# A decoder layer on one core: the expert routing moved from a block of its own into the attention phase, and the sorted rows fetched by GpSimd through a table

## The reference, cut to what matters

```
x = x + attn(layernorm(x))            # 2 x 1024 tokens, width 256, 16 heads of 64, one shared k/v head, causal
x = x + xattn(layernorm(x), ctx)      # 77 context rows for each batch, 16 heads of 16
z = layernorm(x)
logits = z @ w_router                 # 4 experts
e = argmax(softmax(logits))           # one expert for each token
gate, value = split(z @ w_v[e])       # 256 -> 2 x 1024
x = x + (gate * sigmoid(gate) * value) @ w_proj[e]   # 1024 -> 256
```

## Time and profile before

| | |
|---|---|
| time of three runs, median (lowest to highest) | 998.96 us (996.46 to 1001.12) |
| the profiled execution's own time | 1001.04 us |
| its span, first to last instruction | 999.3 us |
| busy share of the span: PE, DVE, ACT, POOL | 88%, 61%, 56%, 20% |
| mean granted TensorE clock | 0.939 of full |

### The profile page before, as it was taken

How to read it: one execution, slowest core, us unless ns; L and a number is a source line. 1 busy time by engine, 2 the same in 40 slices (tenths; PEclk the granted TensorE clock), 3 DMA queues, 4 the chain that set the end, 5 groups by cost and what they waited for, 6 DMA issues and landing times.

```text
span 999.3 us, 14240 instructions
## 1 busy us (share of the span) xinstructions
PE 882.3 (88%) x4366; PEld 669.0 (67%) x4366; DVE 612.9 (61%) x1417; ACT 562.5 (56%) x1112; POOL 203.9 (20%) x220
## 2 busy tenths in 40 slices
PE   4699898999999897999989999999760299999997
PEld 2467676777777675776776777777550178888885
DVE  4667758667858677668766778778766133323231
ACT  1478667677867577667758678768442022222221
POOL 3212321302112121212313020201103401111111
PEclk9699999999999999999989999999955599999999
DMA  8300000020000000000000003200232201010100
GB/s 283 71 1 1 1 1 1 1 85 1 1 2 0 1 2 0 2 1 0 2 1 1 1 1 107 63 1 1 85 127 72 81 1 32 20 32 21 32 17 9
DMA packets 19175, 29.01 MB, mean 29 GB/s; under 512 B 2079, under 2 KB 15648, under 8 KB 19104
## 3 DMA queue, kind: packets, MB, share of 16 engines
q1 hardware_dynamic: 17008, 22.73, 7.5%
q0 software_dynamic: 1680, 4.21, 1.2%
q10 hardware_dynamic: 416, 1.18, 0.3%
HBM read 21.41 MB, written 7.10 MB: 29 GB/s over the span
## 4 chain that ended last, share of the span: by engine, by line
PE 49%; DVE 6%; issue 5%; POOL 3%; ACT 2%; DMA 1%; DVEq 0%; ACTq 0%; POOLq 0%
PE W L1418 7%; PE S L1395 6%; PE O L1395 5%; PE O L1235 3%; PE O L1232 3%; PE S L1217 3%; PE S L1216 3%; PE O L1233 3%; PE W L1306 3%; PE W L1348 3%; PE W L1274 2%; PE W L1328 2%; POOL sorted_rows L700 2%; PE W L1336 1%; PE W L1361 1%
## 5 line engine op out<-in xcount | busy, mean ns | idle before, releaser
L944 DVE TENSOR_TENSOR pl<-pr,ph 128x512 fp32r<-128x512 f32 x288 | 200.2, 698 | 72.4 <-ACT pr L750 64.4
L749 ACT ACTIVATE ph<-S 128x512 fp32r<-128x512 f32 x288 | 173.7, 603 | 107.5 <-PE S L1217 105.2
L750 ACT ACTIVATE pr<-S 128x512 f32<-128x512 f32 x288 | 172.7, 600 | 0.0
L1232 PE MATMUL O<-ph,vhi 128*65 128x512 f32 x288 | 145.1, 504 | 0.0
L1235 PE MATMUL O<-pl,vhi 128*65 128x512 f32 x288 | 116.3, 404 | 8.2 <-DVE pl L944 7.8
L1217 PE MATMUL S<-qT,kT 128*128 128x512 f32 x288 | 115.3, 400 | 0.0
L1216 PE MATMUL S<-qT,kT 128*128 128x512 f32 x288 | 115.0, 399 | 0.0
L1233 PE MATMUL O<-ph,vlo 128*65 128x512 f32 x288 | 114.7, 398 | 0.0
L651 POOL TENSOR_TENSOR rs<-ri,half 128x1 f32<-128x1 f32 x48 | 34.9, 727 | 306.0 <-DVE ri L883 306.0
L1274 PE MATMUL W<-wqkv,zT 128*128 128x384 f32 x192 | 75.5, 527 | 3.8 <-DVE qT L996 1.6
L858 ACT ACTIVATE gate<-S 128x512 f32<-128x512 f32 x38 | 20.6, 596 | 102.8 <-PE S L1395 102.8
(11 more groups left out here) (174 smaller groups left out, 1637.8 us busy)
## 6 DMA issues: line engine op xcount, KB each, us to landing
raw<-in_w_v SPq DMA_DIRECT2D x16, 512.0 KB, 4.0
wps<-in_w_proj SPq DMA_DIRECT2D x4, 1024.0 KB, 10.1
sorted_rows<-pad_row SPq DMA_DIRECT2D x19, 128.5 KB, 4.3
xs<-sorted_rows SPq DMA_DIRECT2D x19, 128.5 KB, 2.0
wqkv<-in_wqkv_t ACTq DMA_DIRECT2D x1, 1152.0 KB, 6.3
wout<-in_wout_t SPq DMA_DIRECT2D x1, 1024.0 KB, 10.0
xall<-in_x SPq DMA_DIRECT2D x1, 1024.0 KB, 10.3
xall<-in_x SPq DMA_DIRECT2D x1, 768.0 KB, 7.8
```

The source lines that it names most:

```text
L749: nc.scalar.activation(ph[:, k % RING, :], S[k % AHEAD][:], ACT.Exp, scale=SIM_SCALE).then_inc(ph_ready, 1)
L750: nc.scalar.activation(pr[:, k % RING, :], S[k % AHEAD][:], ACT.Exp, scale=SIM_SCALE)\
L944: nc.vector.tensor_tensor(pl[:, k % RING, :], pr[:, k % RING, :], ph[:, k % RING, :].bitcast(F32), ALU.subtract).then_inc(pl_ready, 1)
L1232: nc.tensor.matmul(o, vhi[:, vs, 0:DH + 1], ph[:, k % RING, :], start=j == 0, stop=False)
```

## The change

- Routing is done in four groups of tiles: 0 to 7, 8 to 12, 13 and 14, and 15 (`ROUTED`). Two positions behind the last logits of one of the first three groups the planner puts a DVE stage `one_hot`, three further a stage `ranks` (two matmuls on PE, three DVE instructions), and then one `scatter` of a tile on POOL at every third position. The last group is done behind the attention phase.
- `one_hot` breaks ties by weights and keeps a running count of each partition (`before`), one add for each tile. The sum over tiles is now made by PE in the same bank as the ranks.
- Each expert has a region of its own of 2048 rows in `sorted_rows`, so a token's slot is known without the other experts' counts. The buffer grows from 19 to 67 tiles, and all of it is filled with the pad row at the start, in 9 DMAs in place of 19.
- A table `row_i` is made from the counts at the end. With it POOL gathers each sorted tile by an indirect DMA, in place of SP's plain load. `gather(n+2)` stands in POOL's program behind `store(n-3)` and waits for its landing.
- `EARLY` has units 11 to 14 too. Unit 15 is split ahead of ACT's and DVE's waits for the end of the phase.
- Small tensors are kept apart in SBUF, and eight constants are set by DVE at the start.

```diff
+ROUTED = [8, 13, 15, TILES]
+ROUTING = [("one_hot", 2), ("ranks", 3)]
+SCATTER_EVERY = 3
+REGION = TOKENS
+SLOTS = (EXP - 1) * REGION // P + SORTED
+FILL = 8
...
-         7: ("probs_sum", 1), 8: ("probs_turn", 0), 9: ("probs_turn", 2), 10: ("probs_v", 0)}
+         7: ("probs_sum", 1), 8: ("probs_turn", 0), 9: ("probs_turn", 2), 10: ("probs_v", 0), 11: ("probs_v", 0), 12: ("probs_v", 0), 13: ("xo_turn", 0),
+         14: ("xattn_out", 0)}
...
+            if (name, part) == ("logits", EXP - 1) and t + 1 in ROUTED and t + 1 < TILES:
+                r = ROUTED.index(t + 1)
+                for stage, lag in ROUTING:
+                    at += lag
+                    put(at, stage, r, t, order)
+                    load[at][0] += COST[stage][0]
+                for n in range(ROUTED[r - 1] if r else 0, t + 1):
+                    at += SCATTER_EVERY
+                    put(at, "scatter", n, t, order)
...
-        sorted_rows = nc.dram_tensor("sorted_rows", [SORTED * P, ROW], F32, kind="Internal").ap()
+        sorted_rows = nc.dram_tensor("sorted_rows", [SLOTS * P, ROW], F32, kind="Internal").ap()
...
-            for n in range(SORTED):
-                sp.dma_start(sorted_rows[n * P:(n + 1) * P, :], pad_row[:]).then_inc(pad_out, 16)
+            for n in range(0, SLOTS, FILL):
+                m = min(FILL, SLOTS - n)
+                sp.dma_start(sorted_rows[n * P:(n + m) * P, :].rearrange("(n p) d -> p n d", p=P),
+                             pad_row[:].unsqueeze(1).broadcast_to([P, m, ROW])).then_inc(pad_out, 16)
...
-            sp.wait_ge(scattered, 16 * TILES)
-            for n in range(SORTED):
-                if n >= XS:
-                    sp.wait_ge(stored[(n - XS) % 2], 16 * ((n - XS) // 2 + 1))
-                sp.dma_start(xs[:, n % XS, :], sorted_rows[n * P:(n + 1) * P, :]).then_inc(xs_in[n % XS], 16)
...
+            def scatter(t):
+
+                pool.wait_ge(x2_ready, t + 1)
+                pool.indirect_dma_start(out=sorted_rows, out_offset=bass.IndirectOffsetOnAxis(ap=pos_i[:, t:t + 1], axis=0),
+                                        in_=xall[:, t, :], in_offset=None).then_inc(scattered, 16)
...
+                    if name == "scatter":
+                        if part == 0:
+                            pool.wait_ge(pad_out, 16 * N_FILL)
+                        pool.wait_ge(pos_ready, ROUTED.index(t + 1) + 1)
+                        scatter(part)
...
-            pool.wait_ge(pad_out, 16 * SORTED)
-            pool.wait_ge(x2_ready, TILES)
             pool.wait_ge(logit_ready, TILES)
-            nc.gpsimd.iota(tnum_i[:], pattern=[[1, SORTED + 1]], base=0, channel_multiplier=0).then_inc(tile_num, 1)
-            pool.wait_ge(pos_ready, 1)
-            for t in range(TILES):
-                pool.indirect_dma_start(out=sorted_rows, out_offset=bass.IndirectOffsetOnAxis(ap=pos_i[:, t:t + 1], axis=0),
-                                        in_=xall[:, t, :], in_offset=None).then_inc(scattered, 16)
+            nc.gpsimd.iota(tnum_i[:], pattern=[[P, SORTED]], base=0, channel_multiplier=1).then_inc(tile_num, 1)
+            pool.wait_ge(pos_ready, len(ROUTED))
+            for t in range(ROUTED[-2], TILES):
+                scatter(t)
+            pool.wait_ge(act_done, 1)
+            pool.wait_ge(pe_done, 1)
+            pool.wait_ge(rows_ready, 1)
+            pool.wait_ge(scattered, 16 * TILES)
+
+            def gather(n):
+
+                if n >= XS:
+                    pool.wait_ge(stored[(n - XS) % 2], 16 * ((n - XS) // 2 + 1))
+                pool.indirect_dma_start(out=xs[:, n % XS, :], out_offset=None, in_=sorted_rows,
+                                        in_offset=bass.IndirectOffsetOnAxis(ap=row_i[:, n:n + 1], axis=0)).then_inc(xs_in[n % XS], 16)
+
+            gather(0)
+            gather(1)
             for n in range(SORTED):
 
                 pool.wait_ge(f_step, n + 1)
                 nc.gpsimd.tensor_tensor(frs[:], fri[:], half[:, 0:1], ALU.pow).then_inc(f_root, 1)
                 if n >= 3:
                     store(pool, n - 3)
+                if n + 2 < SORTED:
+                    gather(n + 2)
...
-                elif n < 13:
-                    act.wait_ge(side_ready, job_count("scores", 3, TILES - 1))
+                elif n < 12:
+                    act.wait_ge(side_ready, job_count("probs_turn", 2, TILES - 1))
+                    act.wait_ge(sm_ready, 2 * TILES)
+                elif n < 14:
+                    act.wait_ge(side_ready, job_count("probs_v", 0, TILES - 1))
+                else:
+                    act.wait_ge(side_ready, job_count("xattn_out", 0, TILES - 1))
+                    act.wait_ge(x1b_ready, TILES)
...
+            for n in range(EARLY_UNITS, UNITS):
+                weights_high(n)
             act.wait_ge(logit_ready, TILES)
             act.wait_ge(pe_done, 1)
 
             nc.scalar.activation(warm[:], half[:, 0:1], ACT.Silu)
-            for n in range(EARLY_UNITS, UNITS):
-                weights_high(n)
...
+            def one_hot(g):
+                lo, hi = ROUTED[g - 1] if g else 0, ROUTED[g]
+                dve.wait_ge(dconst, 8 + 2 * EXP)
+                r(nc.vector.tensor_reduce(best[:, lo:hi], logits[:, lo:hi, :], AX.X, ALU.max))
+                r(nc.vector.tensor_tensor(eq[:, lo:hi, :], logits[:, lo:hi, :],
+                                          best[:, lo:hi].unsqueeze(2).broadcast_to([P, hi - lo, EXP]), ALU.is_equal))
+                r(nc.vector.tensor_tensor(eq[:, lo:hi, :], eq[:, lo:hi, :],
+                                          order_w[:].unsqueeze(1).broadcast_to([P, hi - lo, EXP]), ALU.mult))
+                r(nc.vector.tensor_reduce(best[:, lo:hi], eq[:, lo:hi, :], AX.X, ALU.max))
+                r(nc.vector.tensor_tensor(oh[:, lo:hi, :], eq[:, lo:hi, :],
+                                          best[:, lo:hi].unsqueeze(2).broadcast_to([P, hi - lo, EXP]), ALU.is_equal))
+                for t in range(lo, hi):
+                    r(nc.vector.tensor_tensor(before[:, t + 1, :], before[:, t, :], oh[:, t, :], ALU.add))
+                dve.sem_inc(one_hot_ready, 1)
+            def ranks(g, job):
+                lo, hi = ROUTED[g - 1] if g else 0, ROUTED[g]
+                dve.wait_ge(side_ready, job + 1)
+                src = W[job % WB][:, 0:(hi - lo) * EXP].rearrange("p (t e) -> p t e", e=EXP)
+                ins = nc.vector.tensor_tensor(rank[:, lo:hi, :], src, oh[:, lo:hi, :], ALU.mult)
+                if g + 1 < len(ROUTED):
+                    ins.then_inc(dve_freed, 1)
+                    dve.wait_ge(dve_freed, freed[job][1])
+                else:
+                    r(ins)
+                r(nc.vector.tensor_reduce(posf[:, lo:hi], rank[:, lo:hi, :], AX.X, ALU.add))
+                nc.vector.tensor_copy(pos_i[:, lo:hi], posf[:, lo:hi]).then_inc(pos_ready, 1)
...
+            one_hot(len(ROUTED) - 1)
+            for n in range(EARLY_UNITS, UNITS):
+                weights_low(n)
             dve.wait_ge(act_done, 1)
             dve.wait_ge(pe_done, 1)
+            ranks(len(ROUTED) - 1, N_SIDE)
+
+            base = W[N_SIDE % WB][:, (TILES - ROUTED[-2]) * EXP:(TILES - ROUTED[-2] + 1) * EXP]
+            r(nc.vector.tensor_scalar(cnt_i[:], base, float(P - 1), None, ALU.add))
             r(nc.vector.tensor_scalar(cnt_s[:], cnt_i[:], 7, None, ALU.arith_shift_right))
             r(nc.vector.tensor_copy(cnt_f[:], cnt_s[:]))
+            r(nc.vector.tensor_tensor(cnt_f[:], cnt_f[:], before[:, 0, :], ALU.subtract))
+            r(nc.vector.tensor_scalar(cnt_f[:], cnt_f[:], float(P), None, ALU.mult))
+            r(nc.vector.tensor_scalar(skip[:], cnt_f[:], -1.0, float(REGION), ALU.mult, ALU.add))
+            for e in range(1, EXP - 1):
+                src = cnt_f if e == 1 else end
+                r(nc.vector.tensor_tensor(end[:, e:e + 1], src[:, e - 1:e], cnt_f[:, e:e + 1], ALU.add))
+            ends = [cnt_f[:, 0:1], end[:, 1:2], end[:, 2:3]]
 
             dve.wait_ge(tile_num, 1)
             r(nc.vector.tensor_copy(tnum[:], tnum_i[:]))
+            for e in range(EXP - 1):
+                r(nc.vector.scalar_tensor_tensor(out=ecmp[:], in0=tnum[:], scalar=ends[e],
+                                                 in1=skip[:, e:e + 1].broadcast_to([P, SORTED]), op0=ALU.is_ge, op1=ALU.mult))
+                r(nc.vector.tensor_tensor(rowf[:], tnum[:] if e == 0 else rowf[:], ecmp[:], ALU.add))
+            r(nc.vector.tensor_copy(row_i[:], rowf[:]))
+            dve.sem_inc(rows_ready, 1)
+            r(nc.vector.tensor_scalar(ecmp[:], tnum[:], ends[0], None, ALU.is_ge))
             for e in range(1, EXP - 1):
+                r(nc.vector.scalar_tensor_tensor(out=ecmp[:], in0=tnum[:], scalar=ends[e], in1=ecmp[:],
                                                  op0=ALU.is_ge, op1=ALU.add))
             r(nc.vector.tensor_copy(expert_i[:], ecmp[:]))
+            dve.sem_inc(table_ready, 1)
...
+            def ranks_of(g, job):
```

(50 more changed lines are left out.)

53 lines of the change are left out of this document (23 added, 30 removed).

## The result

Twenty runs of the changed kernel have a median of 1000.8 us, twenty of the kernel before 998.11 us. The ratio is 1.0027 with a 95% interval of 1.0018 to 1.0036: the change costs 2.7 us, well inside the half per cent named as the limit, but on the other side of zero from the 4.9 us forecast as a gain. One of the twenty, at 2265.09 us, stands apart from all others and is not in the ratio.

What follows compares the result with a forecast made beforehand. PE was taken to bound the FFN loop, with 43.72 us of routing off PE ahead of it. Terms -23.6 + 5.1 + 2.0 + 11.6 = -4.9 us gave 996.1 (994.1 on the median), range 982 to 1004.

Steps and rivals of the forecast that it cites:

- The tail: From 705 us to the last cross-attention add: added one_hot, ranks and scatters cost 5.1 us, plus a 1.2 us slip.
- 1.2 for the weights: Units 11 to 13 split before the last cross-attention add, which slips by 1.2 us; counted within the routing's net gain.
- The loop: FFN loop: gather between store and pow delays fz, PE waits 0.83 us a pass, 14 passes, 11.6 us added.
- the pass absorbs the gather: Rival, FFN loop: short gather hold or earlier landing signal removes the 11.6 us, total 982.5; chance 0.14.
- the gather is dear: Rival, FFN loop: gather holds POOL 1.97 us, PE waits 1.84 us a pass, total 1008.3; chance 0.12.
- The routing: Last add to first up-projection: one scatter left instead of sixteen; first matmul 23.6 us earlier net, stretch itself -24.8.
- The attention phase: Near 554 us: one_hot for tiles 0 to 7 and small matmuls make PE lose 2.0 us, bounds 0.5 and 5.
- The clock: Rival: stalls near 554 and 705 us lower the clock, costing 2.5 and 3.5 us, total 1000; chance 0.16.
- the last tile's output projection: Clock rival's term behind 705 us: this 3.5 us projection takes 3.5 us more at the lower clock.
- the port's rule: Tail scatters: GpSimd cannot write descriptors while DVE holds the shared port; scatters cost the upper price, tail sum 7.1.
- The end: After the last down-projection: no term in the sum, forecast change 0.

Runs made afterwards that it cites:

- Two runs in which only one half of the cost is there: Changed kernel with six xs buffers, so gathers wait on older stores: 990.19 us; kernel before with only a wait for each store's landing added: 997.46 us.
- the second profile: Kernel before, unchanged, profiled a second time: 998.94 us, span 997.2.
- wait alone: Kernel before with POOL waiting for each store's landing before the next pow, gathering nothing: 997.46 us, ratio 0.9998.
- spare DMAs: Kernel before with 19 further indirect DMAs from POOL in the FFN loop, writing to a spare tensor: one execution, 996.5 us, span 994.8.
- the first profile: Kernel before, unchanged, the profiled execution the prediction was read from: 1001.04 us.

## Why the prediction was wrong

**The tail** is the step that failed. I summed what the new stages put in front of the old ones (5.1 us and 1.2 for the weights) and took the order of the old ones as given. The diff adds the new stages' cost to the planner's load, and so moves older stages. Tile 13's probs_v slid by three positions, from right behind the last attention step into the place where DVE did one_hot. With the load uncounted my sum was met within 0.3 us (54.61 for 54.35), with it the tail was 4.2 us longer than the sum. The single terms of the 6.3 weren't measured one by one; without the routing stages the tail fell by 5.5 us where I had 5.1.

**The loop** was right in mechanism and nearly in size: 11.6 us forecast, 11.0 and 10.5 measured against the two profiles of before. The pass is 10.9 us where I had 10.96. The wait for `fz` shows as 0.54 us a pass (7.5 / 14) and not as the 0.8 I named. The pass grows by 0.79 all the same: matmuls that follow one another start 0.23 us apart and the trace gives each 0.40, so the first 0.17 us of a delay don't show as idle. Two runs in which only one half of the cost is there show that it takes both. The rivals "the pass absorbs the gather" and "the gather is dear" are both out: a gather holds POOL for 0.97 us.

**The routing** was right against the same profile: -24.8 forecast, -24.1 measured. A gather lands in 2.77 us, between the 2.17 and 3.04 that I gave as bounds. Against that, POOL started it 0.93 us behind the last table instruction, where I had 0.3. Against the second profile the gain is 22.8 us, and against the mean of the three other profiles with the routing of before (42.39, 42.55, 42.04) it is 22.7. The time of the scatters differs from one execution to another, and I had taken the longest one as the kernel's.

**The attention phase** cost about what I said, and the first row of the table hides it. I take a mark near 508 us, the last matmul of attention step 193 of 288. From it to the last attention matmul the four profiles with the attention phase of before (first, second, wait alone, spare DMAs) take 194.39, 192.76, 194.37 and 191.17 us. They differ in the granted clock behind the mark. First the first profile and the one with spare DMAs, from 510 to 525 us, then the changed kernel where one_hot falls (columns as in the earlier trace rows):

```profile
510.00:525.00 15.00, 14.37 (x64) 11.75 (x65) 7.56 (x18) 5.33 (x12) 2.35 (x3) 0.77 0.00 1
510.00:525.00 15.00, 15.00 (x82) 11.64 (x81) 9.10 (x22) 7.06 (x15) 3.30 (x5) 1.00 0.01 2
```

```profile
550.00:560.00 10.00, 6.95 (x37) 4.67 (x36) 8.98 (x29) 6.13 (x12) 0.00 (x0) 1.00 0.00 0
```

The clock of that window is 0.77, 0.89, 0.77 and 1.00 in the four, and the stretch is 3.2, 1.6, 3.2 and 0 us longer than 191.17. The changed kernel takes 195.06 us with 0.89 there, so 1.6 us of it are the clock's and 2.3 us are the change's, for 2.0 forecast. Its other two profiles (195.05 and 195.17) have 1.00 there and 0.83 from 550 to 560, behind the wait for one_hot: the same 1.6 us in another place. With the load uncounted it is 192.95 us: the stages cost 1.8, the moved order 0.5, and the clock stays at 1.00. In the table the 2.3 us are covered by what differs ahead of the mark: 508.20, 508.59, 507.51 and 507.30 before, 507.23, 506.26 and 505.63 with the change. I leave that difference open.

**The clock** as a rival came in part, and its 1000 us are near the measured time by luck. The fall near 554 us is in two of the three profiles with the changed kernel's attention phase, and costs 1.6 us where I had 2.5. The one behind 705 us is there, behind a hole of 3.7 us that the order had made longer than the 2.3 I named. But the last tile's output projection, which was to take 3.5 us more, took 3.69 us before and after; it was probs_v that took 2.14 more. (The 7.1 that the prediction gives for the tail by the port's rule lies above its own bound: 5.1 with 2.5 in place of 1.0 is 6.6. All seven scatters of the changed kernel's tail held POOL 0.96 to 1.06 us, none the 1.97.)

**The end** wasn't in the sum at all: 1.9 us, of which 1.6 appeared in the run that only adds DMAs started by POOL. The rest is open.

Added up against the first profile: -0.3 + 10.5 - 24.1 + 11.0 + 1.9 = -1.0 us, which is the difference of the spans. Against the second it is +1.1, and the medians say +2.7. The last 1.6 us are which executions were profiled: the second one of before is 0.8 above its median, the one after 0.5 below, and 0.3 lie outside the spans. With the attention phase, the routing and the loop taken as above, the sum is 2.3 + 10.5 - 22.7 + 10.8 + 1.9 = +2.8 us. So of the 7.7 us between the forecast and this sum 4.2 are the tail's, 2.1 the long routing of the profile I read, 1.9 the end, 0.3 the attention phase, and the loop gave 0.8 back. The twenty executions of the kernel before lie between 993.67 and 1001.12 us.

## What to carry to other kernels

When a planner or any list ordered by cost sets the program, an added stage has two prices: its own time, and what moves because it is counted. Read the new order, position by position, before summing. When the stretch to one mark is the same before and after, look at marks on the way: two differences can cover each other, and the granted clock of the same stretch says which part is an execution's chance. When a DMA is moved onto a compute engine's queue, its wait comes with it: put it behind the instruction that others wait for, or give it a buffer more, so that what it waits for is a pass old. A wait that fits and an instruction that fits need not fit together: add them up against the room of the next engine.

## What the runs showed of the hardware that I had not expected

- The end of the program grew with the number of indirect DMAs that GpSimd had started: with 35 of them it is 4.5 us from the last one's issue to the end of the span (three profiles), with 54 of them 5.9 to 6.4 us (eight profiles). From the run that adds only DMAs that is an estimated 0.08 us for each (1.6 / 19).
- A scatter's hold on POOL grows from 0.96 us by what is left of the DVE weight split (`whl`, 128 x 1024, 1.22 us) that runs when it starts, less about 0.12 us: 1.99 us with 1.16 to go, 1.61 with 0.78, 1.01 with 0.18. A scatter that started 0.22 us ahead of a split took 0.96.
- The granted clock fell in the same stretch of the attention phase in some executions of the same instructions and not in others (0.77, 0.89 and 1.00 from 510 to 525 us), for 3.2, 1.6 and 0 us.
- An indirect gather from DRAM costs POOL what a scatter does, 0.97 us of 128 rows of 1028 bytes, and lands 2.8 us after its start.
- The fill of 8.6 MB, from 22 us on, cost nothing that can be seen: with it the mark near 508 us comes at 505.63 to 507.23, before at 507.30 to 508.59.
